# A graph network kernel: 792 of 1563 edge tiles in sorted slots instead of 624

## The reference

```python
h = leaky(x @ W1 + b1) @ W2 + b2                       # per node
e = leaky(edge_attr @ We1 + be1) @ We2 + be2           # per edge
msg = h[src] * e * dot_scale
agg = segment_sum(msg, dst, num_segments=n)
out = x + agg * res_w
x = (out - mean(out)) * rsqrt(var(out) + 1e-5) * ln_g + ln_b
```

## Time and profile before

| | us |
|---|---|
| median of 3 runs | 7039.86 |
| lowest and highest | 7022.78, 7064.93 |
| the profiled execution, its own time | 7057.0 |
| its span | 7055.2 |
| TensorE busy, matmuls (weight loads) | 6114.5 (4219.1) |
| VectorE busy | 5252.9 |
| GpSimd busy | 5154.2 |
| ScalarE busy | 1157.1 |
| mean granted TensorE clock | 0.873 |

### The profile page before, as it was taken

How to read it: one execution, slowest core, us unless ns; L and a number is a source line. 1 busy time by engine, 2 the same in 40 slices (tenths; PEclk the granted TensorE clock), 3 DMA queues, 4 the chain that set the end, 5 groups by cost and what they waited for, 6 DMA issues and landing times.

```text
span 7055.2 us, 128950 instructions
## 1 busy us (share of the span) xinstructions
PE 6114.5 (87%) x43650; PEld 4219.1 (60%) x43651; DVE 5252.9 (74%) x7510; ACT 1157.1 (16%) x1852; POOL 5154.2 (73%) x5411
## 2 busy tenths in 40 slices
PE   7898989999888999887889988889998878988776
PEld 2244446667665566666556667655676665566664
DVE  9974359888757888765788876578877658887765
ACT  0022321111111111111111111111111111111111
POOL 6777757777776777777577777767777776777776
PEclk9965589999878999988899998789998878998887
DMA  4116875455543454544345554444545434545553
GB/s 138 25 40 172 211 194 127 123 131 134 132 111 94 118 129 122 125 123 107 98 119 125 127 125 120 105 102 121 126 123 127 122 94 108 127 125 126 128 126 85
DMA packets 726671, 848.86 MB, mean 120 GB/s; under 512 B 332864, under 2 KB 491856, under 8 KB 724976
## 3 DMA queue, kind: packets, MB, share of 16 engines
q1 hardware_dynamic: 542960, 649.79, 34.0%
q0 software_dynamic: 172288, 175.83, 12.8%
q10 hardware_dynamic: 10752, 14.69, 0.6%
HBM read 727.96 MB, written 111.79 MB: 119 GB/s over the span
## 4 chain that ended last, share of the span: by engine, by line
POOL 65%; issue 22%; PE 6%; DVE 4%; DMA 1%; DVEq 0%; ACT 0%; POOLq 0%; ACTq 0%; SPq 0%
POOL arena L732 57%; POOL slots L719 8%; PE bank L895 1%; DVE arena L1510 1%; PE bank L791 1%; DVE x_packed L1510 1%; PE bank L777 1%; DMA slot_pick<-arena 1%; PE bank L941 1%; DVE arena L1502 1%; PE bank L837 1%; PE bank L931 0%; PE bank L827 0%; PE bank L953 0%; DVE rstd L1444 0%
## 5 line engine op out<-in xcount | busy, mean ns | idle before, releaser
L732 POOL DMA_INDIRECT arena<-h_rows,src x4695 | 4501.8, 959 | 1632.3 <-issue 1426.6
L895 PE MATMUL bank<-w2s,arena 128*128 128x128 f32 x9200 | 1479.9, 325 | 628.1 <-DVE arena L1579 588.1
L895 PEld LDWEIGHTS bank<-w2s,arena 128*128 128x128 f32 x9200 | 1345.7, 231 | 824.2 <-DVE arena L1579 694.5
L953 PEld LDWEIGHTS bank<-arena 112*128 112x128 f32 x8960 | 1068.1, 195 | 432.6 <-issue 408.2
L953 PE MATMUL bank<-arena 112*128 112x64 f32 x8960 | 1145.7, 282 | 0.0
L1116 ACT ACTIVATE arena<-bank,tenth 128x512 f32<-128x512 f32 x590 | 405.3, 687 | 4149.6 <-PE bank L891 4149.5
L1579 DVE TENSOR_TENSOR arena<-arena,bank 128x512 f32<-128x512 f32 x590 | 404.6, 686 | 617.1 <-DMA arena<-h_rows,src 608.7
L719 POOL DMA_INDIRECT slots<-arena,slot_index x624 | 622.3, 997 | 210.3 <-issue 189.5
L891 PE MATMUL bank<-nodes_state,edge_w 64*128 64x512 f32 x1180 | 692.1, 668 | 64.8 <-issue 51.2
L1510 DVE TENSOR_TENSOR x_packed<-bank,slot_rel 128x3968 f32<-128x3968 f32 (+7 forms) x280 | 674.1, 2408 | 19.6 <-issue 19.6
L1510 DVE TENSOR_TENSOR arena<-bank,slot_rel 128x3968 f32<-128x3968 f32 (+7 forms) x280 | 674.5, 2409 | 16.9 <-issue 16.6
(11 more groups left out here) (173 smaller groups left out, 5254.8 us busy)
## 6 DMA issues: line engine op xcount, KB each, us to landing
arena<-slot_pick SPq DMA_DIRECT2D x560, 448.0 KB
arena<-h_rows SPq DMA_DIRECT2D x560, 224.0 KB
nodes_state<-attr_t SPq DMA_DIRECT2D x590, 128.0 KB
arena<-h_rows,src POOLq DMA_INDIRECT x4695
x_packed<-slot_attr SPq DMA_DIRECT2D x560, 128.0 KB
slot_pick<-arena SPq DMA_DIRECT2D x112, 448.0 KB, 3.5
slots<-arena SPq DMA_DIRECT2D x8, 1904.0 KB, 21.4
arena<-slots SPq DMA_DIRECT2D x112, 136.0 KB
```

The lines of the kernel that those rows point to most:

```text
L732: pool.indirect_dma_start(to[0:n, at:at + D], None, table, bass.IndirectOffsetOnAxis(ap=index[0:n, t:t + 1], axis=0)).then_inc(landed(t), 16)
L895: mm = pe.matmul(to[:, j * P:(j + 1) * P], acts[:, j * TILE:(j + 1) * TILE], w2s[:, :], start=True, stop=True)
L953: mm = pe.matmul(slot_ps[:, at:at + D], source_pick[0:ROWS, i % 2, k * TILE:(k + 1) * TILE], source_rows[0:ROWS, i % 2, k * D:(k + 1) * D] ...
```

## The change

792 tiles (99 groups) go into slots and 771 are left to the windows. The low edges are 18 sub-chunks of 44 tiles, two to a *block*; a bucket of a sub-chunk has 64 slots, so a group's tile of 128 rows holds one bucket of each of the block's two sub-chunks, on rows 0 to 63 and 64 to 127. There are 9 blocks of 14 steps, 126 slot groups, with widths of 360, 328, 288, 248, 208, 168, 128, 88 and 48 (1864 in all, not 2176). The sum of a slot group is 16 products of 64 rows into two PSUM banks, not 8 of 128 rows into one. The window sums move to the bank of the window groups' hidden layer.

Edges beyond the 64 slots of a bucket go to spare slots, 32 for each sub-chunk: 5 tiles that are gathered and multiplied as a window group of their own (the seventh, `SPILL_AT`), whose message stays, and which enters the sums at each block's end by two products of 32 rows. So a layer has 98 window groups, 92 of them spread over the 126 steps (`a_at`) and 6 behind them, with a ring of 9. A node tile has 9 steps, not 7.

The ranking runs over 5 phases (four of 4 sub-chunks, one of 2) of 44 rounds, and each of 12 batches also counts the overflow. x is loaded behind it, since its place is now used as scratch. Turning goes block by block.

The core of the diff:

```diff
-SLOTS = 7
+SLOTS = 9
+RING_SLOTS = 9
-CHUNKS = 8
-FIRST_CHUNKS = 4
-CHUNK_TILES = 78
-CAP = 128
-WMAX = 512
+CHUNKS = 9
+SUBS = 2 * CHUNKS
+SUB_TILES = 44
+CAP = 64
+SPILL_CAP = 32
+SPILL_AT = 6
+WMAX = 360
-RANK_STEPS = 6
-FIRST_SLOT = 3
+PHASES = [(0, 4), (4, 8), (8, 12), (12, 16), (16, 18)]
+RANK_CUTS = [[0, 4, 12, 28, 44]] + 4 * [[0, 22, 44]]
+FIRST_SLOT = 2
...
+    def a_before(s):
+
+        return -(-max(s, 0) * IN_LOOP // NB) if s <= NB else min(IN_LOOP + s - NB, GA)
+
+    def a_at(s):
+        return a_before(s) if 0 <= s < STEPS and a_before(s + 1) > a_before(s) else None
+
+    def b_at(s):
+        return s if 0 <= s < NB else None
...
-        sum_ps, win_ps = banks[6], banks[7]
+        sum_ps, win_ps = banks[6:8], banks[2]
```

SP's loads of x, now behind the ranking:

```diff
+            sp.wait_ge(edges_placed, 2)
+            own_wait(sp, "sp")
+            load_x(0, 2, x_head_landed)
+            load_x(2, NT, packed_moved)
```

TensorE, the sums of a slot group:

```diff
+                def chunk_sums(i):
+                    c = i // BG
+                    w = widths[c]
+                    for j in range(TPH):
+                        for side in range(2):
+                            at, k = (2 * j + side) * D, side * TPH + j
+                            for half in range(2):
+                                slots_of = slice(half * D, (half + 1) * D)
+                                mm = pe.matmul(sum_ps[half][side * D:(side + 1) * D, 0:w], msg[slots_of, 1, at:at + D],
+                                               slot_places[i % 2][slots_of, k * w:(k + 1) * w],
+                                               start=(i % BG == 0 and j == 0),
+                                               stop=(ends_chunk(i) and j == TPH - 1 and side == 1))
...
+                    if ends_chunk(i):
+                        pe.wait_ge(spill_picked, l * CHUNKS + c + 1)
+                        pe.wait_ge(spill_msg_ready, l + 1)
+                        own_wait(pe, "pe")
+                        for half in range(2):
...
+                            pe.matmul(sum_ps[half][0:D, 0:w], spill_msg[rows_of, at:at + D], spill_pick[rows_of, 0:w],
+                                      start=False, stop=True).then_inc(sum_ready, 2)
```

TensorE, a step:

```diff
+                def step(s, part):
+                    k = a_at(s + 2)
+                    if k is not None:
+                        pe.wait_ge(added, l * ADDS + adds_before(s) + 1)
...
+                            hidden_of(0, k, GA, attr[:, v, :])
+                    k = b_at(s + 2)
...
+                        hidden_of(1, k, NB, slot_attr_in[:, k % 2, :])
+                    now, m = a_at(s), a_at(s + 1)
...
+                        pe.wait_ge(msg_ready, l * GR + real(now) + 1)
+                    if m is not None:
+                        pe.wait_ge(hid_acted[0], l * GA + m + 1)
+                        edge_out(hidden[:, 0, m % 2, :], e_ps).then_inc(e_ready, 1)
...
+                        pe.wait_ge(slot_msg_ready, l * NB + k + 1)
...
                         edge_out(hidden[:, 1, k % 2, :], slot_ps).then_inc(slot_e_ready, 1)
+                    if now is not None and now != SPILL_AT:
+                        pe.wait_ge(hid_acted[0], l * GA + a_before(s + 3))
+                        window_sums(now)
+                    if b_at(s) is not None:
...
+                        chunk_sums(s)
                     part("middle")
...
+                    if k is not None:
                         pe.wait_ge(slot_e_biased, l * NB + k + 1)
                         gathered(k)
```

VectorE, a step, from behind the two products with source rows:

```diff
+                    m, i = a_at(s + 1), b_at(s + 1)
+                    if m is not None and m != SPILL_AT:
...
+                        one_hot(pick[:, m % 2, :, :], TPG, WIN, rel[:, at:at + TPG])
+                    for side, n, j in ((0, GA, a_at(s + 2)), (1, NB, b_at(s + 2))):
+                        if j is not None:
+                            acted(side, j, n)
+                    if i is not None:
+                        dve.wait_ge(slot_e_ready, l * NB + i + 1)
+                        edge_biased(slot_e, slot_ps[:, :]).then_inc(slot_e_biased, 1)
+                    if m is not None:
+                        dve.wait_ge(e_ready, l * GA + m + 1)
                         edge_biased(e_ps[:, :], e_ps[:, :]).then_inc(e_biased, 1)
...
+                        window_added(s, k)
+                    if ends_chunk(s):
+                        chunk_added(s)
```

VectorE, the places after a batch of the ranking: 14 small operations, and the carry, one add for each round:

```diff
+                    for i in range(end - begin):
+                        ins = dve.tensor_tensor(carry[:, (i + 1) * n:(i + 2) * n], carry[:, i * n:(i + 1) * n],
+                                                over[:, i * n:(i + 1) * n], ALU.add)
+                        prepared(ins)
+                    dve.sem_inc(carried, 1)
...
+                    dve.wait_ge(spill_counted, batch + 1)
...
```

More of the change, by code:

```diff
@@ L730, in gathers @@
                             continue
[L731 removed]
+                        n = last_rows if index is not spill_src and tiles < TPG and t == tiles - 1 else TILE
                         pool.indirect_dma_start(
@@ new lines, in rank_edges @@
+                so_far, batch = 0, 0
+                for ph, (first, end) in enumerate(PHASES):
+                    n = end - first
+                    hot(0, ph, so_far, n)
+                    for i in range(SUB_TILES):
+                        if i + 1 < SUB_TILES:
+                            hot(i + 1, ph, so_far, n)
+                        take(i, so_far, n)
+                        past(i, so_far, n)
+                        total(i, ph, so_far, n)
+                        if i + 1 in RANK_CUTS[ph]:
+                            dve.wait_ge(ranked, so_far + i + 1)
+                            places(ph, max(x for x in RANK_CUTS[ph] if x <= i), i + 1, batch, n)
+                            batch += 1
+                    so_far += SUB_TILES
@@ new lines, in rank_edges @@
+                prepared(dve.scalar_tensor_tensor(gap, edge_dst, 1.0, inside, ALU.add, ALU.mult))
+                for q in range(SUBS):
+                    ph = next(k for k, (first, end) in enumerate(PHASES) if q < end)
+                    at = (SUBS - 1 - q) * SUB_TILES
+                    dst_of, gap_of = (in_phase(v, ph)[:, :, q - PHASES[ph][0]] for v in (edge_dst, gap))
+                    prepared(dve.tensor_tensor(far[:, at:at + SUB_TILES], dst_of, gap_of, ALU.subtract))
+                dve.sem_inc(edges_placed, 2)
@@ new lines, in plan_tiles @@
+                for q in range(SUBS):
+                    ins = dve.memset(due_subs[:, q:q + 1],
+                                     float(next(k for k, at in enumerate(slot_steps) if at >= (q // 2 + 1) * BG)))
+                prepared(ins)
+                prepared(dve.tensor_scalar(plan[:, 1, 0:NS], due_slots[:, :], need, None, ALU.is_lt))
+                prepared(dve.reduce_sum(early, plan[:, 1, 0:NS], axis=X))
+                prepared(dve.tensor_scalar(plan[:, 0, 0:SUBS], chunk_f[0:NT, :], ends, None, ALU.is_lt))
```

665 lines of the change are left out of this document (362 added, 303 removed).

## The result

The kernel after takes 7249.98 us (median of 4 runs, 7245.5 to 7278.5) against 7040.04 us (4 runs) before: a ratio of 1.030, 95% interval 1.026 to 1.035. I had forecast 6805, faster. The profiled execution took 7278.5 us with a span of 7276.4.

The account below looks back on a forecast made before the run. GpSimd's gathers were taken to bound the old layers, TensorE the new. 1303 us before the layers plus 5523 for five gave a 6826 us span, stated as 6805 us, 3.3% faster; range 6640 to 7070.

Parts of the forecast that it names:

- What bounds, and what is late next: In the layers: GpSimd's gathers bound the old kernel; they fall 206 us a layer to 980, leaving TensorE late next.
- Before the layers: Ranking, preparation, x load, plan and slot turning grow by 303 us, so layers begin at about 1303 us, not 1000.
- the seams: Slot turning before the layers: 8 block changes instead of 4, TensorE waiting 5.9 us at each, +24 us.
- Steps, slot sums, block ends: In each layer's loop: steps 659 us, slot sums 206, bank and layout allowance 10, block ends 44.
- The second rival: Slot sums: four products don't run at once, layers lengthen, total 7690 or 7180 us; chance 12%.
- 10 us for the shared bank: Per layer: waits between hidden products and window sums sharing a bank, plus changed layout; bounds 0 and 60 us.
- The change of tiling mode: TensorE between window and slot sums: drains could cost up to 15 us a layer, 76 in all; left out of the sum.
- The node tiles: Tile norms in a layer's loop: 11 of 13 tiles lie there, costed at 100 us a layer.
- 27.4 for three tiles, 9.1 each: Tile price from 28 old-kernel steps: 278.1 us less clean steps and block ends, divided among three tiles.
- the third rival: Steps in the layers: the shared bank makes each a chain, losing 0.5 us, 63 a layer, total 7120 us; chance 12%.
- The rival's sign: TensorE idle before hidden products until VectorE's adds, or before window sums until the leaky step, would show the shared-bank chain.
- The floor of the old order: A layer of the kernel before without its gathers: about 1100 us, so GpSimd stood only some 120 us above TensorE.

Follow-up runs that it names:

- b_few: Kernel before, fetching only two of the eight `h[src]` gathers of every window group: loop 1031 us, layer 1144 us.
- a_few: Kernel after, fetching only 2 of the 8 gathers of every window group, nothing else changed: loop 1114 us, layer 1225 us.
- a_few_own: Kernel after, 2 of 8 gathers, window sums in their own PSUM bank, iota moved to SBUF: loop 1086 us, layer 1188 us.
- a_few_late_early: Kernel after, 2 of 8 gathers, window sums in their own bank, root wait later, tile-slot register reads earlier: loop 1035 us, layer 1132 us.
- a_few_fill2: Kernel after, 2 of 8 gathers, iota in SBUF, unread matmuls (3, 2 and 4) at a tile's three TensorE stops: loop 1063 us, layer 1168 us.
- a_few_fill: Kernel after, 2 of 8 gathers, iota in SBUF, unread matmuls (6, 5 and 9) at a tile's three TensorE stops: loop 1107 us, layer 1217 us.
- a_few_tiles_after: Kernel after, 2 of 8 gathers, the 13 node tiles of a layer moved behind the loop of steps: loop 909 us.

## Why the prediction was wrong

**What bounds, and what is late next: right.** GpSimd is off the path and TensorE on it.

**Before the layers: right.** 1313 us, forecast 1303. Turning takes (1310 - 803) / 126 = 4.02 us each, forecast 3.78 and the seams.

**Steps, slot sums, block ends: right.** 909 us measured, 919 forecast; the slot sums 2.65 us at 360 columns, forecast 2.52. The second rival is dead. The sum holds 10 us for the shared bank, whose waits are 22 us here, so other terms were a little high. The change of tiling mode, up to 15 us a layer by the rule of the Trainium skill (TensorEngine Tiling (Array Packing), Key Properties), doesn't show in TensorE's products: they have no idle time ahead of the slot sums, and the steps sum to less than forecast without it.

**The node tiles: wrong, and this is the step that failed.** I took "27.4 for three tiles, 9.1 each". The stretch held two. Groups by line of the kernel before, VectorE, 1143.93 to 1422.06 us:

```profile
L1444 DVE RECIPROCAL rstd<-std 128x448 f32<-128x448 f32 x2 | 5.9, 2942 | 0.0
```

One reciprocal is one tile. With two, the same sum gives 13.7 each, 151 us a layer instead of 100: five layers 255 us more, 7060 in the terms of the forecast, and the sign is gone. That was to be read before the change. `b_few` confirms the size, 14.2. The 9.1 is no more than TensorE's own products of a tile (8 to 9 us), so it left nothing for waits and slow products.

**What the new order adds: not in the forecast, and in part in the third rival.** 14.2 became 18.4 us a tile, 46 us a layer. I had priced the shared bank by the waits in a clean step, with 10 us. The rival's sign came: in the second layer's loop of the kernel after TensorE idles 22 us before hidden products until VectorE's adds, and 8 before window sums until the leaky step. The longest of these waits lie in a tile, beside the reciprocal (rows above), and a low clock follows them. The bank of its own gives back 28 of the 46 us. What the other 18 are is open. A part may be the wait for the root, 12 us in a loop of `a_few` and at most 1 in one of `b_few`; it and the register reads, with their clock, are worth 51 us in the step from `a_few_own` to `a_few_late_early` (on different chips).

Over 11 tiles, the miscount is 51 us (151 - 100), the half us from 13.7 to 14.2 is 5, and the step from 14.2 to 18.4 is 46: together 102 us a layer. That this equals the whole miss of a layer is chance in part: the steps came out 10 us shorter than forecast, and the start and end of a layer 10 us longer (1217 - 1111 = 106, forecast 96).

**The floor of the old order.** By the same miscount I put it at 1100 us. It is 1144, so the gathers stood 79 us above it, not 120. A change that takes off 206 us of gathers could win 79 a layer at most, some 395 in all, and it added 317 us before the layers and 34 a layer in steps and block ends (909 - 875). Even at the old tile price, 46 us a layer less, it would take about 7020 us by my estimate, level with the 7040 before.

## What to carry to other kernels

Price a piece of work that is woven into a loop as loop with it less loop without it, and count its pieces by an instruction that each has once; don't take it from a stretch of which you haven't counted them. Waits of 1 to 2.7 us on TensorE in a busy loop cost themselves and often slow products behind them, here about as much again in sum; look at the granted clock behind each stop, move register reads behind queued products and a wait to the last point that needs it. When the bound engine is relieved, what it hid is paid in full: measure the floor with that engine's work taken out before the change is built. And when a buffer moves to another memory, compare the mean time of every engine's instructions, not only of those that read it: a run with part of the work left out can hide the price, as 2 of 8 gathers did here.

## What the runs showed of the hardware

- Useless products can pay: 102 matmuls of 256 columns in a loop of 1114 us made it 1063, by a clock of 0.96 instead of 0.91; 226 of them made it 1107 (`a_few_fill2` and `a_few_fill`, on different chips).
- Reading three registers stops TensorE for up to 1.6 us where only the slot sums (0.84 us in a narrow block) are queued ahead of it, 10.8 us in a layer of the kernel after; with six more matmuls ahead 0.4 us of it are left in a loop (`a_few_fill`).
- Four 64 x 64 products run side by side: 32 entries of 360 columns in 2.65 us; at 48 columns 0.68 us, 21 ns an entry, where I had taken no less than 34.
- GpSimd's indirect gather takes 0.95 us beside a VectorE one-hot that reads one input from PSUM, and is held to 0.8 us behind its end (3.80 us) by one that reads both from SBUF.
- The granted clock is at its 1.2 GHz level for 213 us of a loop of the kernel after, and for 40 us of one without tiles (`a_few_tiles_after`).
- Chips differ: the kernel before takes 7040 to 7050 us on two occasions and 10827 to 10959 on four others, with the same program. What differs isn't shown.
